# The token lists of seven experts, made in quarters of TensorE's array with the slot numbers as weights and the rows as the moving side, turned back and added by one more product

## The reference, cut to what matters

```python
h = _layernorm(x) * (1 + cb) + sb                     # x is (4, 512, 256), 2048 tokens in all
probs = softmax(h @ router_w.T)                       # 8 experts
w = _top_p_weights(probs, 0.9)                        # 0 for the experts that a token doesn't keep
for e in range(8):
    g = silu(h @ gate_w[e].T)                         # 256 -> 512
    u = h @ up_w[e].T
    out = out + (g * u) @ down_w[e].T * w[:, e:e+1]   # 512 -> 256
x = x + gb * out
```

## Time and profile before

| | |
|---|---|
| median of three runs | 466.82 us (466.67 to 470.7) |
| the profiled execution | 467.09 us, its span 465.4 us |
| PE busy (matmul) | 436.7 us, 94% of the span, 3466 instructions |
| DVE busy | 331.6 us, 71% |
| ACT busy | 257.5 us, 55% |
| POOL busy | 192.3 us, 41% |
| clock granted to PE | 0.997 of full speed |

### The profile page before, as it was taken

How to read it: one execution, slowest core, us unless ns; L and a number is a source line. 1 busy time by engine, 2 the same in 40 slices (tenths; PEclk the granted TensorE clock), 3 DMA queues, 4 the chain that set the end, 5 groups by cost and what they waited for, 6 DMA issues and landing times. The chain is left out here.

```text
span 465.4 us, 10119 instructions
## 1 busy us (share of the span) xinstructions
PE 436.7 (94%) x3466; PEld 327.1 (70%) x3466; DVE 331.6 (71%) x770; ACT 257.5 (55%) x372; POOL 192.3 (41%) x233
## 2 busy tenths in 40 slices
PE   7979899999999999999999999999899999999992
PEld 6443233343434344448998999999899999999992
DVE  4788977699779977788999676575466485746442
ACT  2276898779777987865433453353253353533330
POOL 4251132032003101022425666666755666666645
PEclk9999999999999999999999999999999999999998
DMA  8702208510011002233364468566448475654534
GB/s 255 255 1 67 72 2 98 84 46 1 1 49 46 0 2 93 92 92 95 117 178 115 96 182 206 88 158 168 81 74 211 95 170 131 134 101 89 88 74 47
DMA packets 30786, 46.02 MB, mean 99 GB/s; under 512 B 3588, under 2 KB 22276, under 8 KB 30728
## 3 DMA queue, kind: packets, MB, share of 16 engines
q0 software_dynamic: 11936, 22.50, 27.2%
q1 hardware_dynamic: 18792, 22.77, 14.9%
HBM read 34.44 MB, written 12.93 MB: 102 GB/s over the span
## 5 line engine op out<-in xcount | busy, mean ns | idle before, releaser
L684 ACT ACTIVATE probs<-psS 128x1024 f32<-128x1024 f32 x128 | 123.8, 1036 | 15.5 <-PE psS L1573 15.4
L1816 PE MATMUL psS<-hs_hi,w_hi 128*128 128x256 f32 x400 | 113.4, 284 | 2.6 <-issue 2.6
L1816 PE MATMUL psS<-hs_lo,w_hi 128*128 128x256 f32 x400 | 112.4, 281 | 0.0
L1816 PE MATMUL psS<-hs_hi,w_lo 128*128 128x256 f32 x400 | 112.3, 281 | 0.0
L529 POOL DMA_INDIRECT out<-y_sel,idx_out x44 | 77.3, 1758 | 32.9 <-DVE y_sel L1364 23.0
L1816 PEld LDWEIGHTS psS<-hs_hi,w_hi 128*128 128x128 f32 x400 | 75.3, 188 | 4.1 <-issue 4.1
L1816 PEld LDWEIGHTS psS<-hs_hi,w_lo 128*128 128x128 f32 x400 | 75.4, 188 | 0.0
L1816 PEld LDWEIGHTS psS<-hs_lo,w_hi 128*128 128x128 f32 x400 | 75.2, 188 | 0.0
L513 POOL DMA_INDIRECT h_sel<-h_rows,idx_in x50 | 51.9, 1038 | 48.7 <-DVE sel L1330 20.2
L1676 PE MATMUL psY<-probs,v_aug 128*32 128x512 f32 x512 | 68.2, 605 | 0.0
L743 ACT ACTIVATE silu_g<-psS 128x512 f32<-128x512 f32 x50 | 29.7, 597 | 60.0 <-PE psS L1816 57.6
(11 more groups left out here) (229 smaller groups left out, 697.6 us busy)
## 6 DMA issues: line engine op xcount, KB each, us to landing
w_in<-gateT SPq DMA_DIRECT2D x8, 512.0 KB
w_in<-upT SPq DMA_DIRECT2D x8, 512.0 KB
w_in<-downT SPq DMA_DIRECT2D x8, 512.0 KB
h_rows<-h_nat SPq DMA_DIRECT2D x4, 528.0 KB
x_all<-x SPq DMA_DIRECT2D x4, 512.0 KB, 5.1
h_rows<-mod_table POOLq DMA_DIRECT2D x4, 512.0 KB
out<-x_all SPq DMA_DIRECT2D x4, 512.0 KB, 2.9
mod_rows<-mod_table SPq DMA_DIRECT2D x3, 512.0 KB, 5.0
```

What stands on the lines that cost most here:

```text
L684: act.activation(probs[:, gk % 4, 2 * pair:2 * pair + 2, :], psS[:, pair, :, :], ACT.Exp, scale=ATT_SCALE / QK_UNIT ** 2).then_inc(probs_d ...
L1816: mm = pe.matmul(ps[:, i * SW:(i + 1) * SW], w, v[:, k, :], start=at == 0, stop=at == 3 * KC - 1)
```

## The change

`one_tile` and `slot_tile` get another layout: the slots stand innermost, so that the 16 slots of one expert, and the 32 of a pair of experts, lie side by side. List 0 is made as before (`list_tokens`, now with 16 contiguous elements moving).

Lists 1 to 7 are made by two functions. `list_in_quarters(e)` also takes 16 products, but with the sides swapped: the weights are the 32 slots of a pair of experts (32 columns), and the 128 rows of `one_row` stream through, 16 elements from one to the next as before. Tile `t` goes to quarter `t % 4` of the array's columns, so four products stand side by side and four such groups follow each other; each quarter adds up the four tiles that it gets. The result is 128 partitions (4 quarters of 2 experts of 16 slots) by 128 rows. ACT copies it out as `list_part` in f16 (`copy_list_parts`). `sum_list(e)` takes one product with `list_part` as weights and `sum_quarters` moving, a constant of ones at 16 places of each quarter: it turns the list back, adds the four quarters and picks the expert. Its result lies where the list lay before, and ACT copies it as before.

The order on PE: `list_in_quarters`, then the 12 down products of `j = 0`, then `sum_list`, then the other 12. For list 1, ahead of the loop, only the four transposes of `turn(4)` stand between the two. POOL makes `sum_quarters` at the start of the kernel, with one memset and four selects. DVE's two operations on `one_tile` are the same in number and size, but read `tile_h` and `token` again and again along the innermost dimension.

```diff
+        sum_quarters = sb("sum_quarters", [P, 3 * TSLOTS], F16)
+        list_part = sb("list_part", [P, P], F16)
+        slot_tile = sb("slot_tile", [P, NT, E, TSLOTS], F16)
...
+        def list_part_ps(e):
+            return (psM if e % 2 == 0 else psY)[:, 1, 256:256 + P]
...
+            pool.memset(sum_quarters[:, :], 0.0).then_inc(quarters_step, 1)
+            for j in range(4):
+                pool.wait_ge(quarters_step, j + 1)
+                pool.affine_select(out=sum_quarters[:, :], in_=sum_quarters[:, :], compare_op=ALU.not_equal, fill=1.0,
+                                   base=TSLOTS - YROWS * j, pattern=[[-1, 3 * TSLOTS]], channel_multiplier=1).then_inc(quarters_step, 1)
...
+            def copy_list_parts(e):
+                act.wait_ge(list_parts_ps, e)
+                act.copy(list_part[:, :], list_part_ps(e)).then_inc(list_part_done, 1)
...
                 if first and e + 2 < E:
+                    copy_list_parts(e + 2)
                     copy_list(e + 2)
...
-                out, of = one_tile[:, :, :, a:z], [P, TSLOTS, NT, z - a]
-                over = lambda v: v[:, :, a:z].rearrange("p (o t) e -> p o t e", o=1).broadcast_to(of)
+                out, of = one_tile[:, :, a:z, :], [P, NT, z - a, TSLOTS]
+                over = lambda v: v[:, :, a:z].rearrange("p t (e o) -> p t e o", o=1).broadcast_to(of)
...
-            def list_tokens(e):
+            def list_in_quarters(e):
                 pe.wait_ge(one_done, EXPERTS0 + e + 1)
                 pe.wait_ge(tiles_listed, 1 if e < EXPERTS0 else 2)
                 if e >= 2:
                     pe.wait_ge(idx_ready, e - 1)
+                two = e // 2 * 2
+                for t in range(NT):
+                    j = t % 4
+                    mm = pe.matmul(list_part_ps(e)[j * YROWS:(j + 1) * YROWS, :],
+                                   one_tile[:, t, two:two + 2, :].rearrange("p e s -> p (e s)"), one_row[:, e % 2, :, t],
+                                   start=t < 4, stop=t >= NT - 4)
+                mm.then_inc(list_parts_ps, 1)
+            def sum_list(e):
+                at = (1 + e % 2) * TSLOTS
+                pe.wait_ge(quarters_step, 5)
+                pe.wait_ge(list_part_done, e)
+                pe.matmul(list_ps(e), list_part[:, :], sum_quarters[:, at:at + TSLOTS], start=True, stop=True).then_inc(lists_ps, 1)
...
                 downs(2, 1, js=(0,))
-                list_tokens(1)
+                list_in_quarters(1)
                 turn(4)
+                sum_list(1)
                 downs(2, 1, js=(1,))
...
                 turn(m + 1)
-                if first and e + 2 < E:
-                    list_tokens(e + 2)
...
-                downs(m - 1, ((e or EXPERTS0) - 1 if first else e) % 3)
+                of = ((e or EXPERTS0) - 1 if first else e) % 3
+                if first and e + 2 < E:
+                    list_in_quarters(e + 2)
+                    downs(m - 1, of, js=(0,))
+                    sum_list(e + 2)
+                    downs(m - 1, of, js=(1,))
```

More of the change, by code:

```diff
@@ L202, in adaln_block @@
         one_row = sb("one_row", [P, 2, P, NT], F16)
-        one_tile = sb("one_tile", [P, TSLOTS, NT, E], F16)
+        one_tile = sb("one_tile", [P, NT, E, TSLOTS], F16)
         hs_hi = sb("hs_hi", [P, KC, SW], F32R)
@@ L447, in _ @@
             small = dict(allow_small_or_imprecise_dtypes=True)
[L448 removed]
+            pool.iota(slot_tile[:, :, :, :], [[0, NT], [0, E], [1, TSLOTS]], base=0, channel_multiplier=0,
                       **small).then_inc(consts, 1)
@@ L790, in last_batch_and_first_items @@
                 gate(3, 1)
+                copy_list_parts(1)
                 round_input(4)
@@ L1202, in early_places @@
                 step(dve.tensor_copy(row0_h[:, :, :], row0_i[:, :, :].rearrange("p t e -> p e t")))
-                step(dve.tensor_tensor(one_tile0[:, :, :, :], slot_tile[:, 0:SLOTS0, 0:TILES0, 0:EXPERTS0],
+                step(dve.tensor_tensor(one_tile0[:, :, :, :], slot_tile[:, 0:TILES0, 0:EXPERTS0, 0:SLOTS0].rearrange("p t e s -> p s t e"),
                                        tile0_h[:, :, :].rearrange("p (o t) e -> p o t e", o=1).broadcast_to(
@@ L1290, in tiles_of_places @@
             def tiles_of_places(a, z):
-                out, of = one_tile[:, :, :, a:z], [P, TSLOTS, NT, z - a]
-                over = lambda v: v[:, :, a:z].rearrange("p (o t) e -> p o t e", o=1).broadcast_to(of)
-                step(dve.tensor_tensor(out, slot_tile[:, :, :, a:z], over(tile_h), ALU.is_equal))
+                out, of = one_tile[:, :, a:z, :], [P, NT, z - a, TSLOTS]
+                over = lambda v: v[:, :, a:z].rearrange("p t (e o) -> p t e o", o=1).broadcast_to(of)
+                step(dve.tensor_tensor(out, slot_tile[:, :, a:z, :], over(tile_h), ALU.is_equal))
                 dve.tensor_tensor(out, out, over(token), ALU.mult).then_inc(tiles_listed, 1)
@@ L1754, in list_tokens @@
                     pe.wait_ge(idx_ready, e - 1)
+                two = e // 2 * 2
[10 more added lines that the diff above has]
+                pe.matmul(list_ps(e), list_part[:, :], sum_quarters[:, at:at + TSLOTS], start=True, stop=True).then_inc(lists_ps, 1)
+            def list_tokens(e):
+                pe.wait_ge(one_done, EXPERTS0 + e + 1)
+                pe.wait_ge(tiles_listed, 1)
                 for t in range(NT):
                     mm = pe.matmul(list_ps(e), one_row[:, e % 2, :, t],
-                                   one_tile[:, :, t, e], start=t == 0, stop=t == NT - 1)
+                                   one_tile[:, t, e, :], start=t == 0, stop=t == NT - 1)
                 mm.then_inc(lists_ps, 1)
@@ L1885, in body_of_item @@
                 turn(m + 1)
-                if first and e + 2 < E:
-                    list_tokens(e + 2)
                 if not first:
                     pe.wait_ge(w_ready, 3 * e + 3)
-                downs(m - 1, ((e or EXPERTS0) - 1 if first else e) % 3)
+                of = ((e or EXPERTS0) - 1 if first else e) % 3
[4 more added lines that the diff above has]
+                    downs(m - 1, of, js=(1,))
+                else:
+                    downs(m - 1, of)
             attention(body)
```

3 lines of the change are left out of this document (1 added, 2 removed).

## The result

| | kernel before | changed kernel |
|---|---|---|
| median of the runs, us | 466.81 (466.67 to 470.7, 4 runs) | 472.19 (470.95 to 472.88, 4 runs) |
| ratio, 95% interval | | 1.0103 (1.0067 to 1.014) |
| profiled execution: time / span, us | 467.09 / 465.4 | 471.58 / 470.0 |
| mean granted clock in it | 0.997 | 0.991 |
| last `turn` before the end (item 25), us | 449.93 | 454.53 |

The forecast was 470.5 with a range of 465.5 to 472.6; the median is inside it, 1.7 us above the forecast. It is above 471.5, where the prediction drew its line of 1%, and the interval of the ratio has 1% inside it. The engine shares did not move (PE 94% of the span in both), so the 4.6 us of span have to be found stage by stage. I compare the starts of the same transposes (`turn`) in both traces.

What follows compares the result with a forecast made beforehand. PE was taken as the bound (94% busy), with a serial loop of POOL and its DMAs ahead of 300.58 us. Terms 0.8 + 0.65 + 1.6 + 0.6 = +3.65 us gave 470.5 us, range 465.5 to 472.6.

Steps and rivals of the forecast that it cites:

- The forecast's own band: End time of the whole kernel if the main forecast holds: 469.5 to 471.8 us, chance 0.50.
- PE's price of a list: PE's time for one list made in quarters: 1.26 us in all, 0.21 more than now.
- entry: On PE, going from `turn` into the quarters: 0.56 us against 0.44 to the list now, 0.12 more.
- sum product: `sum_list` on PE, one product of packed weights and one more switch of form: 0.14 us a list.
- the load behind the block: PE's weight load behind a list, slower than the usual pace of loads: 0.08 us a list.
- The block itself: PE's 16 quarter products: 0.85 us, plus 0.07 for leaving; sign in the timeline, 1.0 us to the first down product.
- rival 1: Quarters on PE go at packed speed, the lists are late all the same: 467.5 us, chance 0.22.
- List 1, +0.8 through PE's sequencer: PE's sequencer, held at `sum_list`, hands out 12 down products late, so the loop's opening register load is late: +0.8 us.
- VectorE's tables, costed at nothing: DVE's large table operations take some 0.95 us more each, hidden ahead of the down products; up to 1 us otherwise.
- Lists 2 and 3, +2.25 together: List 2: late branch on PE, +0.65 us. List 3: POOL waits for ACT's late copy, carried to 300.58, +1.6 us.
- Lists 5 to 7: Late lists on PE, for which POOL doesn't wait: 3 x 0.21 = +0.6 us.
- Rival 3: Clearly slower: the fetch behind list 2 also comes too late for PE, 1.1 to 1.7 us more, 471.9 us; chance 0.15.

Runs made afterwards that it cites:

- experiment 8: The changed kernel with `one_row` in the other order, the 128 elements that a product streams side by side in place of 16 apart: 477.46 us, ratio 1.0236.
- experiment 9: The changed kernel, quarters kept, with `one_row` in pairs of token tiles and `one_tile` in pairs of experts, made two experts at a time: 465.98 us, ratio 0.9981.
- experiment 1: The changed kernel without quarters, sum and ACT's extra copy, so only the new table layout and constants stay: 471.24 us, ratio 1.0076.
- experiment 2: The changed kernel with the large table of tiles made two experts at a time, six short VectorE operations in place of two long: 471.21 us, ratio 1.0092.
- experiment 5: The kernel before with lists 2 to 7 made by the same 16 products, but later, between the two halves of the down products: 469.29 us, ratio 1.0052.
- experiment 12: The kernel before with only `one_row` put in pairs of token tiles, so list weights lie 2 elements apart in place of 16: 463.76 us, ratio 0.9922.
- experiment 3: The changed kernel with `one_tile` in pairs of experts, two neighbours innermost, made two experts at a time: 472.72 us, ratio 1.0129.
- experiment 11: The changed kernel with both tables in pairs, but lists made by the 16 products of the kernel before, no quarters or sums: 465.78 us, ratio 0.9974.
- experiment 4: The changed kernel with quarters for lists 5 to 7 alone, lists 1 to 4 made by the 16 products as before: 470.75 us, ratio 1.0075.

## Why the prediction was right, and where only by its sum

The range held. The class given the best chance, within 1% of the kernel before (0.70), is left open: the ratio is 1.0103 with an interval on both sides of 1.01, and the median lies above the 471.5 that the prediction named as the line; the class beyond it had 0.27. The forecast's own band, 469.5 to 471.8, was missed by 0.4 us. Of the steps, by the order of the sum:

- **PE's price of a list: right in kind, a little small.** Forecast 0.21 us more, measured 0.30. The parts: entry 0.12 forecast, 0.53 - 0.44 = 0.09 measured; sum product 0.14 and 0.12; the load behind the block 0.08 and 0.11. The block itself, from its first product to the first down product, is 1.03 us, as I had named it among the signs (1.0), but in the sum I had put 0.85 + 0.07 = 0.92 beside the old 0.97: those 0.11 us are most of what was missing. The choice of the slow end for elements 16 apart was right, and for the reason given: experiment 8 shows 0.34 with packed rows, so rival 1 (467.5), which gave that pace to rows 16 apart, had the wrong one. The Trainium skill's rule in "SBUF — State Buffer", section "Door 1: The DMA port swizzle", on two hits for each line of 16 bytes pointed to the right bound, and experiments 8 and 9 agree with it.
- **List 1, +0.8 through PE's sequencer: wrong mechanism.** I reckoned 0.9 us for handing out 12 down products behind the sum. The loop's register load started 1.6 us behind the list's start, 1.5 before, and within 0.1 us of the sum at 252.83, though 12 down products stand between them: handing out cost next to nothing there. Behind list 2 the branch came 2.0 us behind the list's start, not 2.4. So the 1.8 us of rows 7 and 12 can't be the time to hand products out; that it is a wait for data is likely, but no row separates it.
- **VectorE's tables, costed at nothing: this is the step that failed.** I took 0.95 us more for each large operation (0.80 measured) and then asked only who reads the result. The down products indeed never waited for it. But I put the cost on VectorE alone; the engine that paid was GpSimd, held at its copy and its fetch, and the fetch had no slack: 1.52 us (experiments 1 and 2). The sum had nothing for this.
- **Lists 2 and 3, +2.25 together: mechanism right, size too large.** ScalarE's copy of list 3 at 3.46 us (3.37 forecast; the terms as printed add to 3.35) and GpSimd's wait of 1.97 us ("past 2") show the mechanism. The `turn` of 300.58 came at 304.11 (303.6 named), but 2.34 us of that were there at item 5, and only 1.19 came behind it. 0.85 us of GpSimd's lateness went into the wait of 1.49 us that the loop already had the earlier trace rows: I had read that wait as part of a serial loop, and here it was slack. Experiment 5 prices the lateness at 1.06, with a landing 0.87 us quicker in it.
- **Lists 5 to 7: 0.6 forecast, 1.07 measured**, 0.9 of it PE's own.

So 0.8 + 2.25 + 0.6 = 3.65 forecast stands against 1.52 + 1.19 + 1.07 = 3.78 measured: two errors of opposite sign, and that they nearly cancel is luck. Rival 3 (the fetch comes too late for PE behind list 2) was near in kind, one list off and for another cause. The remaining 0.8 us of the span are there before list 1, most likely by the clock at the start; between the medians the difference is 5.4 us, and the rest of it is the scatter of a few runs.

## What to carry to other kernels

Before the form of a product is changed, look at how its operands lie: here a step of 2 in place of 16 elements of 16 bits, and nothing else, took the loads from 167 to 100 ns and the list from 0.97 to 0.49 us (experiment 12), more than packing the array gave in any kernel here. When an order of dimensions is changed for one engine, price it on every engine that writes or reads the table, and for VectorE ask besides which GpSimd instructions will meet the longer operation. Two innermost neighbours can serve both: each side then reads or repeats pairs.

## What the runs showed of the hardware

- VectorE, 16-bit operands, two inputs from SBUF: 2048 elements in 1.22 us when the broadcast operand has two or more neighbours innermost, 2.28 us when it repeats one element along the innermost dimension (experiments 8 and 9); 512 elements in 0.42 and 0.69 (experiments 3 and 2). In the kernel before 512 elements took 0.63 us: there too two neighbours lie innermost, but table, constant and numbers all come as 2 elements out of 8. The Trainium skill, "VectorE: DVE Perf Modes", section "What auto-detection actually checks", asks for a step of one in every operand for the doubled rate; a repeated element has step 0, and the traces agree. The 0.63 isn't explained by it.
- GpSimd's iota of 2048 elements: 2.53 us for 128 inner runs of 16 (the changed kernel), 3.82 for 256 runs of 8 (the kernel before), 12.35 for 1024 runs of 2 (experiment 3).
- TensorE, f16: the groups of four products in quarters, 128 elements moving, follow each other at 0.22 us with elements 16 apart and at about 0.05 with elements packed or 2 apart (experiments 8 and 9); a chain of 16 full products with 16 elements moving goes at 0.06 us a product with weights 16 apart, 0.03 and 0.025 with weights 2 apart (experiments 12 and 11).
- A wait of PE of about 1.5 us was followed by some four microseconds mostly at the lower clock (1.2 GHz) in two traces of four (experiments 1 and 4, 264 to 268 us), which cost 1.2 us besides the wait. It was not so in the changed kernel and in experiment 8 (waits of 1.64 and 1.54 us). Why the one and not the other stays open, as does what lowers the clock at 11 to 14 us or at 198 to 204 us in eleven of the twelve experiments' traces.
